# Norm weights applied at a copy, weight splits placed in other batches, GpSimd work in halves and the expert choice spread over steps

## What is computed

```python
x = x + tanh(g_xattn[1]) * _L1_xattn_ref(_layernorm(x), ctx_2048, w_qkv, w_proj, b_proj)   # 16 heads of 16
x = x + tanh(g_ffn[1]) * _L1_ffn_ref(_layernorm(x), norm_w, w1, w3, w2, gate_w, a1, b1, a3, b3, a2, b2)
# _L1_ffn_ref:
t = x * rsqrt(mean(x * x) + EPS) * norm_w
probs = softmax(t @ gate_w.T)                       # 8 experts
topw, topi = top_k(probs, 2); topw = topw / sum(topw)
h1 = t @ w1.T + SCALING * (t @ a1.T) @ b1.T         # low-rank part for each expert; h3 alike
act = silu(h1) * h3
out_e = act @ w2.T + SCALING * (act @ a2.T) @ b2.T  # then the weighted sum over the two chosen experts
```

## Time and profile before

| | |
|---|---|
| Time, median of 3 runs (lowest to highest) | 1524.48 us (1524.08 to 1525.07) |
| Profiled execution: time; span | 1539.73 us; 1538.0 us |
| Busy share of the span: TensorE, VectorE, ScalarE, GpSimd | 89%, 57%, 46%, 36% |
| Mean granted TensorE clock | 0.948 |
| Feed-forward of layer 1 (1229 to 1538 us): TensorE busy | 294.51 of 309.00 us |

### The profile page before, as it was taken

One profiled execution on the slowest core, in us unless ns is written; L12 is line 12 of the kernel. 1 busy time (PEld: TensorE's weight loads), 2 busy tenths in 40 slices (PEclk: granted clock), 3 DMA queues, 4 the chain that ended last, 5 costly groups with the idle time before them and its releaser, 6 DMA issues. The chain is left out here.

```text
span 1538.0 us, 31436 instructions
## 1 busy us (share of the span) xinstructions
PE 1365.9 (89%) x8188; PEld 1074.9 (70%) x8189; DVE 870.8 (57%) x2394; ACT 704.9 (46%) x1879; POOL 560.3 (36%) x622
## 2 busy tenths in 40 slices
PE   4988997999999999999166998898997899999998
PEld 3876665777777777777044666676775699999997
DVE  7969971333333333333446676666668576666666
ACT  2533232444444444444044776666775544444443
POOL 1002554333333333331657666866434111111110
PEclk8968998999999999999568999999998999999999
DMA  4034103777565656643432112221021000000000
GB/s 103 0 90 134 32 11 104 217 211 231 173 209 177 186 161 203 211 116 91 130 104 79 46 45 60 66 69 51 9 64 48 8 15 15 15 14 14 14 7 15
DMA packets 98384, 136.40 MB, mean 89 GB/s; under 512 B 19899, under 2 KB 82307, under 8 KB 98275
## 3 DMA queue, kind: packets, MB, share of 16 engines
q1 hardware_dynamic: 55315, 61.41, 13.4%
q0 software_dynamic: 15456, 48.62, 11.8%
q10 hardware_dynamic: 27504, 25.05, 4.8%
HBM read 103.01 MB, written 32.01 MB: 88 GB/s over the span
## 5 line engine op out<-in xcount | busy, mean ns | idle before, releaser
L1240 PE MATMUL ps<-wgu,xT 128*128 (+1 forms) x892 | 308.0, 469 | 2.3 <-ACT xT L1023 1.0
L762 POOL DMA_INDIRECT xg<-n_rows,idx x191 | 180.6, 945 | 296.7 <-DVE wS L2054 208.5
L1240 PE MATMUL ps<-wdn,hT 88*128 (+1 forms) x892 | 227.8, 380 | 3.8 <-DVE hT L2060 2.9
L2189 DVE TENSOR_REDUCE nmx<-ps 128x1 f32<-128x333 f32 x256 | 127.2, 498 | 132.0 <-PE ps L1240 120.1
L1240 PEld LDWEIGHTS ps<-wgu,xT 128*128 128x128 f32 x892 | 154.8, 193 | 53.9 <-issue 5.1
L1118 ACT ACTIVATE pD<-ps,nmx 128x333 f32<-128x333 f32 x256 | 138.8, 545 | 99.9 <-DVE nmx L2189 79.5
L2057 DVE TENSOR_TENSOR hC<-sg,ps 128x176 f32<-128x176 f32 x191 | 64.5, 338 | 179.3 <-ACT sg L1074 168.8
L1240 PEld LDWEIGHTS ps<-wdn,hT 88*128 88x128 f32 x892 | 153.0, 190 | 18.1 <-issue 3.8
L1532 PE MATMUL ps<-ident,pD 128*128 128x128 f32 x768 | 131.3, 282 | 36.3 <-DVE pT L2195 28.4
L2060 DVE COPY hT<-ps 88x256 f32<-88x256 f32 x191 | 80.4, 421 | 136.5 <-issue 86.4
L779 POOL DMA_INDIRECT yg<-y_rows,slotG x128 | 123.5, 965 | 80.6 <-issue 29.6
(11 more groups left out here) (302 smaller groups left out, 3063.7 us busy)
## 6 DMA issues: line engine op xcount, KB each, us to landing
y_rows<-yC ACTq DMA_DIRECT2D x191, 128.0 KB
wgu<-in_wgu SPq DMA_DIRECT2D x64, 352.0 KB
wdn<-in_wdn SPq DMA_DIRECT2D x64, 176.0 KB
xg<-n_rows,idx POOLq DMA_INDIRECT x191
kraw<-in_kD SPq DMA_DIRECT2D x8, 308.0 KB
x<-in_x SPq DMA_DIRECT2D x4, 512.0 KB, 4.5
n_rows<-nB SPq DMA_DIRECT2D x4, 512.0 KB, 3.4
xg<-n_rows SPq DMA_DIRECT2D x16, 128.0 KB, 2.1
```

The lines of the kernel that those rows point to most:

```text
L762: pool.indirect_dma_start(out=xg[:, b % XS, :], out_offset=None, in_=n1_rows, in_offset=bass.IndirectOffsetOnAxis(ap=idx[:, b:b + 1], axis ...
L1240: return pe.matmul(o, lhsT, rhs, start=start, stop=stop, **kw)
L2189: dve.tensor_reduce(nmx[:, k:k + 1], ps[:, score_bank(k), 0:NK1], AX, ALU.max, negate=True).then_inc(d_mx, 1)
```

## The change

The norm weight is no longer multiplied into `w1`, `w3` and the gate weights on GpSimd (`scale_gates` goes), but into the turned norm when VectorE copies it out of PSUM (`e_copy`). `split` makes the low part in two halves, and `sum_rows` the first sum in two halves. Pieces 2 to 5 are split inside batch 5, one behind each `spread_rec`, in place of one after each of batches 1 to 4; pieces 6 to 11 are split two at a time inside batch 6, in place of one at a time and two at its end. `select` for 12 tiles has eleven parts at eleven steps in place of five, and the `HEAD_*` steps come later. The late `select` is cut in other places over chunks 4 to 7.

```diff
-        SELECT_AT = (1, 3, 4, 5, 6)
-        HEAD_HIGH_AT, HEAD_HALF_AT, HEAD_TURN_AT, HEAD_RANKS_AT, HEAD_LOW_AT, HEAD_COPY_AT = 4, 13, 16, 19, 21, 23
+        SELECT_AT = (1, 3, 4, 5, 6, 7, 9, 10, 12, 13, 14)
+        HEAD_HIGH_AT, HEAD_HALF_AT, HEAD_TURN_AT, HEAD_RANKS_AT, HEAD_LOW_AT, HEAD_COPY_AT = 4, 19, 21, 23, 25, 27
-        LATE_TURN_AT, LATE_LOGITS_AT, LATE_SELECT_AT, LATE_EXP_AT = 1, 2, 4, 5
+        LATE_TURN_AT, LATE_LOGITS_AT, LATE_EXP_AT = 1, 2, 5
+        LATE_SELECT_AT = {4: (0,), 5: (1, 2, 3), 6: (4, 5, 6), 7: (7, 8, 9, 10)}
...
-                if b in (2, 3):
-                    load_raw(b + 2)
+                if b == BATCH - 3:
+                    load_raw(4)
+                    load_raw(5)
                 if b == BATCH - 2:
                     sp.wait_ge(k_red, 2 * NT)
-                    for k in range(6, 10):
+                    for k in range(6, 12):
                         load_raw(k)
                 if b == BATCH - 1:
-                    load_raw(10)
-                    load_raw(11)
...
-                if k < 6:
-                    own.link(pool.tensor_scalar(raw, raw, nwP[:, (k - 2) % DC:(k - 2) % DC + 1], None, ALU.mult))
...
                 own.link(pool.tensor_copy(high, raw))
-                pool.tensor_tensor(low, raw, high.bitcast(F32), ALU.subtract).then_inc(r_done, 1)
...
+                def part(ap, j):
+                    return ap[:, j:j + 1, :] if 6 <= k < 10 else ap[:, j * RAW // 2:(j + 1) * RAW // 2]
+                own.step(pool.tensor_tensor(part(low, 0), part(raw, 0), part(high, 0).bitcast(F32), ALU.subtract))
+                pool.tensor_tensor(part(low, 1), part(raw, 1), part(high, 1).bitcast(F32), ALU.subtract).then_inc(r_done, 1)
...
-                own.link(pool.tensor_tensor(yg[:, q, 0:4, :], yg[:, q, 0:4, :], yg[:, q, 4:8, :], ALU.add))
+                own.step(pool.tensor_tensor(yg[:, q, 0:2, :], yg[:, q, 0:2, :], yg[:, q, 4:6, :], ALU.add))
+                own.link(pool.tensor_tensor(yg[:, q, 2:4, :], yg[:, q, 2:4, :], yg[:, q, 6:8, :], ALU.add))
...
-                    scale_gates()
...
-                    if b == BATCH - 2:
-                        split(6 + g)
+                    if b == BATCH - 3:
+                        split(2 + g)
+                    if b == BATCH - 2 and g < NG1 - 1:
+                        split(6 + 2 * g)
+                        split(7 + 2 * g)
...
-                if 1 <= b <= 4:
-                    split(b + 1)
...
-                    split(10)
-                    split(11)
...
-                pe.wait_ge(e_w, 1)
+                pe.wait_ge(ld_e, 16 * 5)
...
-                dve.tensor_copy(nTs[:, :, r * P:(r + 1) * P], ps[:, bank, at:at + D].rearrange("p (c n) -> p c n", c=DC)).then_inc(e_in, 1)
+                dve.wait_ge(ld_e, 16 * 5)
+                dve.tensor_tensor(nTs[:, :, r * P:(r + 1) * P], ps[:, bank, at:at + D].rearrange("p (c n) -> p c n", c=DC),
+                                  nwP[:].unsqueeze(2).broadcast_to([P, DC, P]), ALU.mult).then_inc(e_in, 1)
```

More of the change, by code:

```diff
@@ L336, in bass_flamingo @@
             sem(n) for n in ("d_s", "d_mx", "d_exp", "d_pt", "d_eva", "d_evd", "d_pv", "d_au", "d_rec", "d_rx", "d_den", "d_att", "d_pr", "d_x"))
-        e_w, e_in, e_st, e_sel = (sem(n) for n in ("e_w", "e_in", "e_st", "e_sel"))
+        e_in, e_st, e_sel = (sem(n) for n in ("e_in", "e_st", "e_sel"))
         f_ld = [sem(f"f_ld{r}") for r in range(2)]
@@ L2120, in select @@
                     norms.link(dve.tensor_tensor(pr_, pr_, of_tile(s1_), ALU.mult))
+                gt_, eq_ = (a[:, 0:nt * E1, :] for a in (gt, eq))
+                other = pr_.unsqueeze(2).broadcast_to([P, nt, E1, E1])
+                this = pr_.unsqueeze(3).broadcast_to([P, nt, E1, E1])
                 if part == 2:
+                    norms.link(dve.tensor_tensor(gt_.rearrange("p (t i) j -> p t i j", t=nt), other, this, ALU.is_gt))
+                if part == 3:
+                    norms.link(dve.tensor_tensor(eq_.rearrange("p (t i) j -> p t i j", t=nt), other, this, ALU.is_equal))
+                if part == 4:
                     dve.wait_ge(const_ready, 4)
[L2123 to L2129, removed]
+                    e3 = eq_.rearrange("p (t i) j -> p t (i j)", t=nt)
+                    norms.link(dve.tensor_tensor(e3, e3, triE[:].rearrange("p i j -> p (i j)").unsqueeze(1).broadcast_to([P, nt, E1 * E1]), ALU.mult))
+                if part == 5:
+                    norms.link(dve.tensor_tensor(gt_, gt_, eq_, ALU.add))
+                if part == 6:
+                    norms.link(dve.tensor_reduce(rk_, gt_, AX, ALU.add))
+                if part in (7, 8):
+                    sel_, w_ = ((first, w0), (second, w1))[part - 7]
+                    norms.link(dve.tensor_scalar(sel_, rk_.rearrange("p (t e) -> p t e", t=nt), float(part - 7), None, ALU.is_equal))
+                    norms.link(dve.tensor_tensor(lg_, pr_, sel_, ALU.mult))
+                    norms.link(dve.tensor_reduce(w_, lg_, AX, ALU.add))
+                if part == 9:
                     norms.step(dve.tensor_tensor(s1_, w0, w1, ALU.add))
@@ L2133, in select @@
                     norms.link(dve.reciprocal(s1_, s1_))
+                if part == 10:
                     norms.step(dve.tensor_tensor(less, second, first, ALU.subtract))
@@ L2371, in f_batch @@
                             e_take(BATCH - 1, 7, 0)
[L2372 to L2377, removed]
+                        for part in LATE_SELECT_AT.get(f, ()):
+                            select(LATE_E, 1, gtL, eqL, part)
                     if f == OUT_AT and not (isinstance(b, int) and b == 0):
```

## The result

| | before | after |
|---|---|---|
| Median (lowest to highest), 20 runs each | 1526.80 us (1522.91 to 1531.99) | 1522.15 us (1517.74 to 1526.04) |
| Ratio after / before, 95% interval | | 0.9968, 0.9959 to 0.9977 |
| Profiled execution: time; span | 1539.73; 1538.0 us | 1518.49; 1516.7 us |

The change makes the kernel 4.65 us faster, where 14.6 were forecast. The time of 1522.15 us lies above the forecast range of 1504 to 1518. In the rows PE is TensorE, DVE is VectorE, ACT is ScalarE, POOL is GpSimd and SPq is SyncE's queue.

A forecast was written before the change was run, and what follows sets the result against it. TensorE, busy 89% of the span, was taken to set the end, so only its waits counted. Terms -11.6 + 0.5 + 3.0 - 7.1 + 0.6 = -14.6 us took 1524.5 to about 1510 us, range 1504 to 1518.

The forecast's parts named there:

- Splits inside batch 5: Layer 1 attention, batch 5: one split behind each reciprocal copy just fits before the power operation's result is needed; +0.5 us.
- Batches 2 to 4: Layer 1 attention: without splits between batches 1 to 4, these three take batch 1's 49.2 us each; -11.6 us.
- Norm weight at the copy: VectorE's copy from PSUM becomes a multiplication of the same length, and GpSimd's multiplications go; 0 us.
- Halves: GpSimd's 1024-wide sums become two 512-wide ones, cutting what VectorE can be held from 2.4 to 1.3 us; 0 us by itself.
- Two splits at a time in batch 6: Batch 6: two splits delay the power operation, so VectorE's Newton steps and then TensorE wait; +3.0 us, bounds 1 and 5.
- Choice of experts with the head: Batch 7: choice spread over 14 steps loses its stretched VectorE instructions, -7.1 us; later head steps add 0.6 us.
- The base: Whole kernel: the 15 us between profiled execution and runs' median carried over unchanged, 1524.5 us before the change.
- The moved splits hold VectorE every time: Rival, batches 5 to 7: ten moved splits hold VectorE, costing 26 us against 18.1 saved; about 1532 us, 3%.
- The split was not what made batches 2 to 4 slow: Rival: sums and gathers keep GpSimd late; only two named waits go, 7.9 us, and batch 7 saves 3.5; 1516.5 us, 17%.
- The power operation is late more dearly: Rival: its lateness costs +5 us in batch 6 and +3 in batch 5; 1514.5 us, 10%.
- code loading in batch 0: Sign of a wrong forecast: code loading in batch 0, marked as remote waits, shifts with the program's layout; no size given.

The follow-up runs named there:

- e10: The changed kernel with SyncE's raw-weight loads 4 and 5 ahead of batch 7's context load, as e2 but on the last chip: 1512.02 us, 0.991 of before.
- e2: The changed kernel with SyncE's loads of raw weights 4 and 5 moved ahead of batch 7's context load: 1526.53 us, 0.9917 of before.
- e5: The changed kernel, unedited, run again on a second chip: span 1518.4 us, ratio 0.997 to before.
- e8: The kernel before with only the norm weight moved to the copy, splits left where they were: 5.5 us faster, 0.9963 of before.
- e7: The kernel before, unedited, profiled on the chip of e5 and e8: span 1525.1 us.
- e12: The kernel before with only the splits' low parts and the first sum made in two halves: 1.0008 of before.
- e6: e2's kernel plus a pause, two GpSimd multiplications of the gate weights by 1.0 in batch 0: 1509.87 us, 0.9887 of before.
- e9: The same kernel as e6 (loads first, pause in batch 0), run again on the chip of e10: 1510.01 us, 0.9892 of before.
- e4: The kernel before with only the spread choice of experts and the later head steps: 2.5 us faster, 0.9984 of before.
- e3: e2's kernel with the power operation ahead of the splits behind the second reciprocal copy of batches 5 and 6: 0.9938 of before.
- e1: The kernel before, unedited, profiled once more on the first chip, beside e2 to e4: span 1536.4 us.
- e11: e9's kernel with GpSimd's 1024-wide rest of the low-rank product in two halves, feed-forward part: 1508.81 us, 0.9888 of before.

## Why the prediction was wrong

**The step that failed** is "Splits inside batch 5", with "+0.5 us, bounds 0 and 3". It took for granted that the raw weights are there, and worked out only GpSimd's own time. The diff moved `load_raw(4)` and `load_raw(5)` on SyncE's queue behind the wait in `load_ctx(7)`; that queue was not read. A load is due before its first reader, and the row that shows it is the queue's own. The cost falls into batch 6, whose clock of 0.94 against 0.97 in e10 is part of it: 57.8 - 51.0 = 6.8 us, of which 5.4 are the wait for `recX` and 1.4 is TensorE's busy time (48.1 against 46.7). Put right by e2's edit, the gain is 13.8 us on two chips (e2, e10; by their ratios 12.8 and 13.7), against 14.6 forecast. So 8 to 9 of the 10 us that were missing lie in this step. The profile shows 6.8 of it; the rest I did not find in its rows. The profiles are of single executions, 3.7 us under the median (after) and 2.7 us over it (e10).

**Point by point**, on the chip of e5 to e8, where the kernel before has a profile of its own (e7):
- Batches 2 to 4: -13.5 (156.8 to 143.3), forecast -11.6, its high bound 13.7. They run at 47.8 us each, faster than batch 1 and than batch 5 (48.3). The mechanism was right, the size too small. Half of it is the multiplications (e8), and some is the clock: TensorE's busy time falls by 3.2 us (138.65 to 135.45), and one of the three batches of e7 runs at a clock of 0.97, none of e5's.
- Norm weight at the copy: 0 on VectorE, right, 0.413 us for 0.414.
- Halves: 0 by themselves, right in time (e12, 1.0008). The reason given, that what VectorE can be held falls from 2.4 to 1.3 us, is wrong where two halves follow each other: the addition is held for both, 2.93 us (e12). In the changed kernel it is short because the sums are over before it.
- Batch 5 itself: 0.0, with the loads first 0.2 (e6), forecast +0.5. The late power operation there costs nothing seen once the loads are in time.
- Two splits at a time in batch 6: forecast +3.0. The wait is 3.19 us, and the power operation starts 6.0 us after the copy, as said. Batch 6 is +2.9 at a clock of 1.00 (e6) and +4.5 at 0.97 (e9, e10). The estimate of 1.0 us for 384 columns was met (1.00).
- Choice of experts with the head: -6.3, forecast -6.5. Alone it gives -4.4 in the batch (e4) and -2.5 in the time by its ratio; the rest needs the last splits out of batch 7's way.
- The feed-forward part: forecast 0, measured 323.0 and 323.4 us against 322.2 (e7). The same programs differ there by 1.8 (e10 and e9), so no loss is shown.
- The base: the span's difference was carried over from a profile of a slower chip. It did no harm to the difference, since e10 and e2 gain the same 13.8 us.

**The rivals.** "The moved splits hold VectorE every time" is out: in batches 5 and 6 of e10 only the four `nS` instructions are longer, 0.68 us in the mean for 0.41, 1.1 us in all, and in e3 three Newton steps. "The split was not what made batches 2 to 4 slow" is out by e8 and e5. "The power operation is late more dearly" has the right place for the loss and not its cause. A late transfer was not among them. The last sign of being wrong, "code loading in batch 0", is not shown by any run: that the waits marked remote are code loading stands in no row. The profile has six transfers on its instruction queues in batch 0 with the stops (e1, e2) and without them (e5, e7, e10), and none of them falls into the 5 us stops. The changed kernel has no wait marked remote of over 1 us in its two profiles (after, e5).

**What the runs leave open.** How much moving the splits alone gives was not tried. The parts that were, e4, e8 and e12, add up to 2.5 + 5.5 - 1.2 = 6.8 us; the changed kernel gains 4.65, and 13.8 with the loads first. If the parts add, which was not tried either, the move as it was made is worth about -2 us, and some 7 in the better order. Whether the pause in batch 0 has an effect beside the chance of the clock is open too: batch 1 is at 0.97 in three of the six profiles without GpSimd's multiplications in batch 0 (after, e8, e10) and in none of the eight with them. That is a hint, and no proof.

**A version that beats both kernels** is e2's edit on the changed kernel (0.991), with the pause 0.9887 and 0.9892, with the rest in halves too 0.9888: 1508.81 us against 1525.77 for before. The last three can't be told apart.

## What to carry to other kernels

When a piece of work moves earlier, find the transfer that feeds it on the queue that issues it, and check every wait that stands ahead of that transfer in program order: a wait that cost nothing for a late reader can be the longest of the stage for an early one. When two engines share a lock for whole instructions, taking work from in front of a reader only helps if it does not then run beside that reader; count what runs beside the next steps, and not only what stands ahead of them. Halving a holding instruction need not shorten the hold: the other half held the next instruction here (e11), or the same one on top of the first half (e12).

## What the runs showed of the hardware

- **The clock falls or not behind the same wait.** Behind one of 3.2 us TensorE ran part of the next 8 us at 1.2 GHz in e9 and not in e11. A dip costs 1.6 us, and batches 1, 6 and 7 show it in some profiles and not in others: all three in e10, none in e6, 4.8 us together, more than the change's own 4.65 us. In the kernel before, batches 2 and 4 take 53.4 us at 0.97 in e1 and 51.7 at 1.00 in e7.
- **Chips differ in stops of three engines.** In batch 0 on the chip of e1 to e4, while rows are gathered, TensorE, VectorE and ScalarE stand nearly still for some 5 us at a time. In e1 from 817.4 to 822.4 they are busy for 0.64, 0.03 and 0.00 us, and GpSimd for 4.35. The profile marks ScalarE's and VectorE's waits there as remote; the row below is from e1, the two behind it are from e2. On the other two chips no such wait is over 1 us. Batch 0 takes 124.4 us in e1 and 131.4 in e2, against 117.1 to 118.9 in e5 to e12. So the profile of e2 has 7 us there that the changed program does not have on the others. The medians of e2 and e10 gain the same 13.8 us over before, so it is not shown that ordinary executions have them too. The cause was not tried.

```profile
822.42 0.48 ACT L1125 COPY pT<-ps 128x384 f32<-128x384 f32 x1 [5.07 <-remote]
```

```profile
824.36 0.48 ACT L1117 COPY pT<-ps 128x384 f32<-128x384 f32 x1 [5.06 <-remote]
830.18 0.58 ACT L1092 CAST kqh<-ps 128x512 fp32r<-128x512 f32 x1 [4.81 <-remote]
```
